# Mamba projections of a fused transformer layer: four z tiles moved into the state scans, and the order of the dt stage changed

## The reference

```python
xz = x @ in_proj_w.T
xp, z = jnp.split(xz, 2, axis=-1)
xpad = jnp.pad(xp, ((0, 0), (d_conv - 1, 0), (0, 0)))
xc = sum((xpad[:, k:k + L, :] * conv_w[:, k] for k in range(d_conv))) + conv_b
xc = jax.nn.silu(xc)
x_dbl = xc @ x_proj_w.T
dt = jax.nn.softplus(x_dbl[..., :dt_rank] @ dt_proj_w.T + dt_proj_b)
Bm = x_dbl[..., dt_rank:dt_rank + d_state]
Cm = x_dbl[..., dt_rank + d_state:]
def step(h, ts):
    dt_t, B_t, C_t, u_t = ts
    dA = jnp.exp(dt_t[..., None] * A)
    h = h * dA + (dt_t * u_t)[..., None] * B_t[:, None, :]
    y = jnp.einsum('bds,bs->bd', h, C_t)
    return (h, y)
...
y = ys.transpose(1, 0, 2) + xc * D
y = y * jax.nn.silu(z)
return y @ out_proj_w.T
```

## Time and profile before

| | |
|---|---|
| median of 3 runs | 9802.43 us (9801.89 to 9803.57) |
| the profiled execution | 9804.51 us, span 9802.8 us |
| TensorE matmul, busy | 7878.8 us, 80% |
| VectorE, busy | 7618.6 us, 78% |
| ScalarE, busy | 4259.3 us, 43% |
| GpSimd, busy | 4330.9 us, 44% |
| mean granted TensorE clock | 0.909 of full |

### The profile page before, as it was taken

The page is one execution under the profiler, slowest core; times in us unless marked ns, Lnnn a source line. Parts: engine busy times, 40 slices in busy tenths (PEclk is TensorE's granted clock), DMA queues, the critical chain, the costliest instruction groups (busy, mean ns, idle before and its releaser), DMA issues. The chain is left out here.

```text
span 9802.8 us, 98275 instructions
## 1 busy us (share of the span) xinstructions
PE 7878.8 (80%) x31796; PEld 3811.3 (39%) x31796; DVE 7618.6 (78%) x11589; ACT 4259.3 (43%) x7991; POOL 4330.9 (44%) x2631
## 2 busy tenths in 40 slices
PE   5788787887978878788887878878788787887977
PEld 2343343433434334343343434434343243432434
DVE  5787977779687696876878778787787877878777
ACT  2535435254442543525435254353534535345353
POOL 1451825418154271632726336262361724518245
PEclk8898998989989898898989889899898988989989
DMA  3020020200202002020020200102011020100202
GB/s 78 1 51 3 5 49 1 52 1 9 45 0 53 1 9 45 0 53 1 13 41 0 53 1 22 32 0 53 1 28 26 0 53 1 38 15 5 49 1 52
DMA packets 265191, 229.93 MB, mean 23 GB/s; under 512 B 26947, under 2 KB 237635, under 8 KB 264531
## 3 DMA queue, kind: packets, MB, share of 16 engines
q1 hardware_dynamic: 264678, 223.50, 10.6%
HBM read 151.60 MB, written 70.25 MB: 23 GB/s over the span
## 5 line engine op out<-in xcount | busy, mean ns | idle before, releaser
L639 POOL TENSOR_TENSOR arena<-arena 128x1024 f32<-128x1024 f32 x1024 | 2435.6, 2389 | 1312.4 <-DVE arena L1041 862.4
L778 ACT ACTIVATE PS<-arena,Aneg 128x512 f32<-128x512 f32 x2048 | 1410.5, 691 | 1628.1 <-DVE XNT L1081 883.6
L704 ACT ACTIVATE arena<-PS 128x512 f32<-128x512 f32 (+3 forms) x3072 | 1286.9, 508 | 861.4 <-PE PS L1249 856.9
L1363 PE MATMUL PS<-XNT,identf 128*128 128x512 f32 x2048 | 1012.2, 618 | 320.9 <-POOL XNT L622 320.9
L948 DVE TENSOR_REDUCE pm<-PS 128x1 f32<-128x512 f32 (+3 forms) x1728 | 1051.2, 663 | 271.5 <-PE PS L1228 169.6
L601 POOL TENSOR_SCALAR_AFFINE_SELECT arena<-arena 128x512 f32<-128x512 f32 x512 | 329.6, 644 | 2063.6 <-ACT arena L704 2063.6
L1225 PE MATMUL PS<-arena 96*128 96x512 bf16 (+3 forms) x3072 | 1105.5, 385 | 106.3 <-PEq L1447 49.4
L1363 PE MATMUL PS<-arena,identf 128*128 128x512 f32 x2048 | 1025.6, 625 | 161.9 <-DVE arena L1057 161.9
L1249 PE MATMUL PS<-arena 99*128 99x512 bf16 (+3 forms) x3072 | 894.5, 332 | 5.9
L1348 PE MATMUL PS<-arena,sel 96*128 96x512 bf16 x1664 | 513.7, 391 | 389.0 <-DVE arena L1057 319.5
L686 ACT ACTIVATE XNT<-PS 128x512 f32<-128x512 f32 x320 | 187.4, 597 | 1335.2 <-PE PS L1184 1334.5
(11 more groups left out here) (143 smaller groups left out, 13086.2 us busy)
## 6 DMA issues: line engine op xcount, KB each, us to landing
pieces_scratch<-arena SPq DMA_DIRECT2D x816, 64.0 KB
arena<-pieces_scratch SPq DMA_DIRECT2D x68, 384.0 KB, 10.0
arena<-pieces_scratch SPq DMA_DIRECT2D x85, 256.0 KB, 10.5
arena<-in_x SPq DMA_DIRECT2D x17, 1024.0 KB, 5.6
U<-in_x SPq DMA_DIRECT2D x17, 1024.0 KB, 5.6
arena<-pieces_scratch SPq DMA_DIRECT2D x136, 128.0 KB, 10.2
out<-X SPq DMA_DIRECT2D x64, 256.0 KB, 5.7
arena<-pieces_scratch SPq DMA_DIRECT2D x17, 768.0 KB
```

The source lines that it names most:

```text
L639: nc.gpsimd.tensor_tensor(DB[:, n % 2], DTU[:, j, half(th)].unsqueeze(1).to_broadcast([P, SP2, TH]), BB[:, SP2 * sg:SP2 * (sg + 1), :], AL ...
L704: A(PT[s % len(PT)][:, hh, 0:w], bank(t_bank(n))[:, 0:w], ACT.Exp, scale=DH ** -0.5)\
L778: A(bank(da_bank(m)), DT[:, j, half(th)], ACT.Exp, scale=Aneg[:, j, SP2 * sg + ss:SP2 * sg + ss + 1]).then_inc(S("dA"), 1)
L1363: ins = MM(bank(4 + jt % 2), identf[:, :], HS[k % len(HS)][:, ss, :], start=False, stop=sg == NSG - 1 and ss == SP2 - 1)
```

## The change

Z tiles 4 to 7 are no longer made ahead of the scans. TensorE makes them in steps 9, 12, 15 and 18 of the scans' loop, each after the sum of the unit before, in banks 6 and 7. ScalarE makes the tanh of each in its step n + 1, behind the two dA, and VectorE the silu in its step n + 2, behind the scans. As `in_proj` needs XNT that long, HS 2 and 3 get memory of their own (HS2), for which the selectors shrink to one column each, read 128 times. The dt stage is reordered: x projection of half 0, its four dt tiles, x projection of half 1, its four. The Ln of the first tile is an instruction of its own.

```diff
-        sel = sb("sel", [3 * 2 * DS, 2 * DS, P], BF16)
+        sel = sb("sel", [3 * 2 * DS, 2 * DS], BF16)
+        HS2 = sb("HS2", [P, 2 * SP2 * TH])
...
-            return k % 4 if k < 4 else (k + 2) % 4
+            return k % 4 if k < 4 else 6 + k % 2
...
-        DT_BANK = (6, 7, 0, 1, 2, 3, 6, 7)
+        DT_BANK = (6, 7, 0, 1, 2, 3, 0, 1)
+
+        SIDE_AT = {9: 4, 12: 5, 15: 6, 18: 7}
...
-                    pool.wait_ge(S("dtl"), nth + 1)
+                    pool.wait_ge(S("dtl"), nth + 2)
...
+            split_bc(0)
+            abs_dt(0)
+            exp_dt(0)
+            split_bc(1)
+            abs_dt(1)
+            exp_dt(1)
             spread_b(0)
-            for th in range(NTH):
-                own.wait(own.n - NTH + 1 + th)
-                A(DT[:, :, half(th)], DT[:, :, half(th)], ACT.Ln, bias=1.0).then_inc(S("dtl"), 1)
-            for k in range(4, ND * NTH):
-                tanh_z(k)
+            ln_dt(0, slice(0, 1))
+            ln_dt(0, slice(1, ND))
+            ln_dt(1, slice(0, ND))
...
                     if m < SP2:
-                        act.wait_ge(S("z"), 5 + m)
+                        act.wait_ge(S("drl"), ND + 1 + m)
...
+                if n - 1 in SIDE_AT:
+                    tanh_z(SIDE_AT[n - 1])
...
             times_u(0)
-            for k in range(4, ND * NTH):
-                silu_z(k)
-            dve.wait_ge(S("z"), ND * NTH)
...
                 dve.wait_ge(S("ys"), NSG * (jt + 1))
+                dve.wait_ge(S("z"), NTH * j + th + 1)
...
+                if n - 2 in SIDE_AT:
+                    silu_z(SIDE_AT[n - 2])
...
                 if n >= 6:
-                    pe.wait_ge(S("dab"), n - 5)
-                    pe.wait_ge(S("drl"), n - 5)
+                    pe.wait_ge(S("dab"), n - 3)
+                    pe.wait_ge(S("drl"), n - 3)
...
+            def selector(s):
+                return sel[:, s:s + 1].to_broadcast([3 * 2 * DS, P])
...
-            pe.wait_ge(S("bc"), NTH)
+            x_proj(0)
+            for n in range(ND):
+                dt_proj(n)
+            x_proj(1)
+            pe.wait_ge(S("bc"), 1)
+            pe.wait_ge(S("drl"), 2)
+            spread_b(0)
+            for n in range(ND, ND * NTH):
+                dt_proj(n)
+            spread_b(1)
             pe.wait_ge(S("drl"), ND * NTH)
-            pe.wait_ge(S("dab"), ND * NTH)
-            for k in range(4):
-                if k % 2 == 0:
-                    spread_b(k // 2)
-                in_proj(ND * NTH + 4 + k)
-            pe.wait_ge(S("z"), ND * NTH)
...
+                    if b_copied(n + 1) == NSG:
+                        pe.wait_ge(S("z"), ND * NTH)
...
+                if n in SIDE_AT:
+                    if SIDE_AT[n] == 4:
+                        pe.wait_ge(S("Be"), NSG)
+                    elif SIDE_AT[n] >= 6:
+                        pe.wait_ge(S("z"), SIDE_AT[n] - 1)
+                    in_proj(ND * NTH + SIDE_AT[n])
```

More of the change, by code:

```diff
@@ L189, in build @@
         two = [t.rearrange("p (n s t) -> p n s t", n=2, s=SP2)
-               for t in (view(28688, 2 * SP2 * TH), XNT[:, :, :].rearrange("p c t -> p (c t)"))]
+               for t in (view(28688, 2 * SP2 * TH), HS2[:, :])]
         HS = [two[0][:, 0], two[0][:, 1], two[1][:, 0], two[1][:, 1]]
@@ L197, in build @@
         TZ, TM = (view(at, 1024).rearrange("p (n t) -> p n t", n=2) for at in (28688, 13312))
+        TZ2 = view(31248, 1024).rearrange("p (n t) -> p n t", n=2)
         TC = view(24592, 4096).rearrange("p (j t) -> p j t", j=ND)
@@ L299, in _ @@
                 nc.vector.tensor_copy(mask1[:, :], mst[:, 0, :])
-                nc.vector.tensor_copy(sel[:, :, :], stage[0:3 * 2 * DS])
+                nc.vector.tensor_copy(sel[:, :], stage[0:3 * 2 * DS, :, 0])
                 nc.vector.tensor_scalar(ipw[:, :, DI:], ipw[:, :, DI:], 0.5, None, ALU.mult)
@@ L420, in dve_c, with tanh_of @@
             return not pool_c(n)
+        def tanh_of(k):
+            return (TZ if k < 4 else TZ2)[:, k % 2, :]
         def z_bank(k):
-            return k % 4 if k < 4 else (k + 2) % 4
+            return k % 4 if k < 4 else 6 + k % 2
         def row_bank(stage, i):
             return i % MB if stage == 2 else i % (2 * MB)
-        DT_BANK = (6, 7, 0, 1, 2, 3, 6, 7)
+        DT_BANK = (6, 7, 0, 1, 2, 3, 0, 1)
+        SIDE_AT = {9: 4, 12: 5, 15: 6, 18: 7}
         OUT_AT = [44 + 4 * i for i in range(NT // NTH)]
@@ L719, in tanh_z @@
                     act.wait_ge(S("z"), k - 1)
-                A(TZ[:, k % 2, :], bank(z_bank(k)), ACT.Tanh).then_inc(S("tz"), 1)
+                A(tanh_of(k), bank(z_bank(k)), ACT.Tanh).then_inc(S("tz"), 1)
             def tanh_c(m):
@@ L741, in scalar_program, with split_bc @@
             tanh_z(3)
-            for th in range(NTH):
+            def split_bc(th):
                 act.wait_ge(S("xpr"), th + 1)
@@ L745, in scalar_program, with abs_dt, exp_dt, ln_dt @@
                 A(BCP[:, half(th)], bank(4 + th)[0:SR, :], ACT.Copy).then_inc(S("bca"), 1)
[L746 to L753, removed]
+            def abs_dt(th):
+                for j in range(ND):
+                    n = th * ND + j
+                    act.wait_ge(S("dtp"), n + 1)
+                    A(DT[:, j, half(th)], bank(DT_BANK[n]), ACT.Abs, bias=dtb[:, j:j + 1]).then_inc(S("dab"), 1)
+            def exp_dt(th):
+                act.wait_ge(S("dab"), ND * (th + 1))
+                A(DT[:, :, half(th)], DT[:, :, half(th)], ACT.Exp, scale=-1.0).then_inc(S("dte"), 1)
+            def ln_dt(th, js):
+                act.wait_ge(S("dte"), th + 1)
+                A(DT[:, js, half(th)], DT[:, js, half(th)], ACT.Ln, bias=1.0).then_inc(S("dtl"), 1)
             def spread_b(k):
@@ L996, in silu_z @@
                 dve.wait_ge(S("tz"), k + 1)
-                V_.scalar_tensor_tensor(out=Z[:, m, half(th)], in0=TZ[:, k % 2, :], scalar=1.0, in1=bank(z_bank(k)),
+                V_.scalar_tensor_tensor(out=Z[:, m, half(th)], in0=tanh_of(k), scalar=1.0, in1=bank(z_bank(k)),
                                         op0=ALU.add, op1=ALU.mult).then_inc(S("z"), 1)
@@ L1024, in vector_program, with relu_dt @@
                     .then_inc(S("bc"), 1)
[L1025 to L1030, removed]
+            def relu_dt(th):
+                for j in range(ND):
+                    n = th * ND + j
+                    dve.wait_ge(S("dtp"), n + 1)
+                    dve.wait_ge(S("dab"), n + 1)
+                    V_.tensor_scalar(DTU[:, j, half(th)], bank(DT_BANK[n]), dtb[:, j:j + 1], 0.0, ALU.add, ALU.max)\
+                        .then_inc(S("drl"), 1)
+            for th in range(NTH):
+                split_bc(th)
+                relu_dt(th)
             def times_u(jt):
@@ L1291, in tensor_program, with x_proj @@
                 in_proj(n)
-            for th in range(NTH):
+            def x_proj(th):
                 for j in range(ND):
@@ L1296, in tensor_program, with dt_proj @@
                 ins.then_inc(S("xpr"), 1)
-            for n in range(ND * NTH):
+            def dt_proj(n):
                 th, j = divmod(n, ND)
@@ L1310, in spread_b @@
                     pe.wait_ge(S("Be"), k)
+                if k == 1:
+                    pe.wait_ge(S("bc"), NTH)
                 for ss in range(SP2):
-                    ins = MM(bank(6 + ss), sel[:, SP2 * sg + ss, :], BCP[:, half(th)], start=True, stop=True)
+                    ins = MM(bank(6 + ss), selector(SP2 * sg + ss), BCP[:, half(th)], start=True, stop=True)
                 ins.then_inc(S("Bg"), 1)
-            pe.wait_ge(S("bc"), NTH)
-            pe.wait_ge(S("drl"), ND * NTH)
-            pe.wait_ge(S("dab"), ND * NTH)
-            for k in range(4):
-                if k % 2 == 0:
-                    spread_b(k // 2)
-                in_proj(ND * NTH + 4 + k)
-            pe.wait_ge(S("z"), ND * NTH)
+            x_proj(0)
[8 more added lines that the diff above has]
+            spread_b(1)
+            pe.wait_ge(S("drl"), ND * NTH)
             pe.wait_ge(S("diag"), ND)
@@ L1347, in tensor_program @@
                         for ss in range(SP2):
-                            ins = MM(bank(c_bank(ss)), sel[:, DS + SP2 * sg + ss, :], BCP[:, half(th)],
+                            ins = MM(bank(c_bank(ss)), selector(DS + SP2 * sg + ss), BCP[:, half(th)],
                                      start=True, stop=True)
```

1 line of the change is left out of this document (removed), and 2 rows, old and new, of the table names.

## The result

| | before | after |
|---|---|---|
| median | 9802.6 us (9801.9 to 9803.6) | 10019.8 us (10017.4 to 10021.1) |
| ratio | | 1.0222, 95% interval 1.0209 to 1.0235 |
| profiled execution | 9804.5, span 9802.8 | 10021.1, span 10019.4 |

A forecast was written before the change was run, and what follows sets the result against it. The dt stage was taken as a latency chain through ScalarE, later scans as VectorE-bound with GpSimd close behind. Per sequence 0.1 + 11.1 + 2.7, rounded to 13.8 us, x 16 = 221 on 9802.4: 10023 us, range 9905 to 10085.

The forecast's parts named there:

- The main term: Scans with side tiles: dA stands behind a tanh waiting for TensorE's projection; with the silu, 11.1 us per sequence.
- tile 4's wait: Scan 11 waits for dA behind tanh 4, whose projection follows unit 8's sum on TensorE: +3.0 us.
- silu 4, tile 5's wait: VectorE's silu of tile 4 adds 0.6 us; scan 14 then waits through unit 11's product, TensorE and ScalarE: +1.6.
- tile 6's wait, with silu 5: Scan 17 waits through GpSimd's product of unit 14, TensorE and ScalarE: +2.5 us, silu of tile 5 hidden in it.
- silu 6, tile 7's wait: Silu of tile 6 adds 0.6 us; from unit 17's product TensorE and ScalarE add a wait of 2.2.
- sum of 0.1: ScalarE's path in the dt stage: -2.5 us (tanh moved), +0.2 (Ln piece), +2.4 (later second Exp), per sequence.
- The clock term of 2.7: TensorE at half clock after idling in the scans' stalls: +1.6 us at tile 5, +1.1 at tile 7; between 0 and 5.
- (a): Rival: the stalls in the scans as forecast, but no clock loss there: 9982 us; chance 0.12.
- (b): Rival: TensorE at full clock in the dt stage, 9974 us, chance 0.10; opposite, dt 4 to 7 at half, 10075, 0.05.
- (c): Rival: z projections held back the early scans; units 0 to 7 fall from 33.0 towards 26.8 us: 9927 us; chance 0.07.
- (d): Rival: side tiles hide fully in the scans, projection ready when ScalarE reaches tanh 4: 9754 to 9793 us; chance 0.07.
- (e): Rival: side tiles stall the scans more as halves of the clock chain up, 17 us per sequence: 10075 us; chance 0.09.

The follow-up runs named there:

- e2: New dt order alone, with z tiles 4 to 7 made ahead of the scans as in the kernel before: 9858.3 us, ratio 1.0080.
- e3: The changed kernel with the dt stage in the order of before, side tiles and early tanh as changed: 9963.5 us, ratio 1.0165.
- e11: The changed kernel with the dt matmuls over 112 rows instead of 16, zero weights for 96 of them: 9965.6 us, ratio 1.0166.
- e9: The kernel before with one added VectorE multiply per sequence, in unit 40 of the scans: 9802.7 us, ratio 1.0000.
- e4: The changed kernel with the old dt order and the side tiles' tanh and silu one unit later: 9745.3 us, ratio 0.9942 to before.
- e1: The changed kernel with ScalarE's tanh and VectorE's silu of each side tile one unit later: 9898.1 us, ratio 1.0101 to before.
- e5: e4 with the two x projections interleaved, both halves made for each block: 9746.4 us, ratio 0.9944 to the kernel before.
- e8: e5 with the dt matmuls over 112 rows instead of 16: 9720.4 us, ratio 0.9917 to the kernel before.
- e7: The kernel before with the dt matmuls over 112 rows instead of 16, zero weights for 96 of them: 9749.2 us, ratio 0.9946.
- e10: The kernel before with three added VectorE multiplies per sequence in unit 40, each waiting for the one before: 9910.3 us, ratio 1.0111.

## Why the prediction was right

**The main term: right in mechanism, place and size.** Forecast and measured starts of the scans (the first kind of sequence: what each step adds to the delay against the kernel before):

| step of the sum | forecast | measured |
|---|---|---|
| tile 4's wait | 3.0 | 2.85 |
| silu 4, tile 5's wait | 0.6 + 1.6 | 0.6 + 1.6 |
| tile 6's wait, with silu 5 | 2.5 | 3.15 |
| silu 6, tile 7's wait | 0.6 + 2.2 | 0.4 + 2.4 |
| silu 7 | 0.6 | 0.6 |
| sum | 11.1 | 11.6 |

I had called the silu of tile 5 hidden. It was hidden in the sense that scan 17 hangs on scan 14 through GpSimd, but the chain was 0.6 us longer than I had counted, 0.5 of it because TensorE came to it at half clock. Its sum of unit 14, 1.88 us at full:

```profile
445.67 2.38 PE L1409 MATMUL PS<-HS,identf 128*128 128x512 f32 x4
```

**The dt stage: right in half of the sequences.** The sum of 0.1 and its course hold in sequences 0, 2, ...: clock down under dt 2, up in the middle of x projection 1, first scan at +0.1. The last Abs and the first dA (as the earlier trace rows):

```profile
358.36 0.69 ACT L760 ACTIVATE arena<-PS,dtb 128x512 f32<-128x512 f32 x1 [1.02 <-PE PS L1340]
...
368.62 0.69 ACT L760 ACTIVATE arena<-PS,dtb 128x512 f32<-128x512 f32 x1 [0.40 <-PE PS L1340]
...
378.58 1.30 ACT L800 ACTIVATE PS<-arena,Aneg 128x512 f32<-128x512 f32 x2
```

The last Abs ends 17.9 us after the first read; 17.6 was forecast. In the others the clock was at half under dt 0 to 3 and most of x projection 1, +2.2. My bound of 3.3 for half clock had it under dt 4 to 7, which ran at full in both kinds (982.5 to 989.1 us at 1.00), and it was for all sequences at once; I had not seen that the sequences could differ. e2 confirms the late start (2.6, as forecast with the Ln piece), e3 the gain of the moved tanh (2.7 where 2.5 less 0.2 for Ln had been forecast). Two slips stand in the sum itself: the second Exp is 2.5 us late and enters as 2.4, and 13.9 is rounded to 13.8. Together they are 0.2 us per sequence, 3 us of the forecast.

**The clock term of 2.7: right in sum, wrong in place.** It was put into the stalls of tiles 5 and 7. In the changed kernel half-clock stretches followed three of TensorE's four idle gaps of 2.3 to 2.7 us there, but their records were mostly off the chain; 0.5 us was lost, at tile 6. In e11, where the stretches fall elsewhere in the scans, the stalls cost 2.4 us more, close to the 2.7. The clock's real share came in at the dt stage with the early scans (0 and 2.8, mean 1.4) and at the MLP and behind it (+2.6 and -0.6, mean 1.0), with 0.4 regained in the late scans between: together with the 0.5 about 2.5. That the clock made all of the part behind the MLP is argued from where its stretches lie, not shown. So part of the closeness of 10023 to 10020 is luck. e9 shows how much: the kernel before with 1.6 us more on the path of each sequence measures the same.

**The rivals.** (a), no clock loss, would have been right about the stalls and wrong about the sum. (b) is out in both forms: the first four dt tiles ran in part or in whole at half in both kinds, and dt 4 to 7 at full. (c) is out: units 0 to 7 took 32.9 us, and 33.5 in the second kind. (d) is out as the change stands: the projection ended 3 us too late, as its point of decision said. With a unit more of time and the old dt order it is what happens: e4 measured 9745, 9 us below the range given for (d). (e) was too high: the four waits cost what they cost one by one (9.6 us idle, 9.8 regained in e1).
The selector read as one column loads in 99 ns like the one before, at the lower bound that I took:

```profile
L1353 PEld LDWEIGHTS PS<-arena,sel x512: 97/99/152, 362.8 to 9777.3; 96*128 96x128 bf16 x171
```

The early start of unit 0 on GpSimd, for which Ln was cut, brought nothing, as the first scan waits for dA.

## What to carry to other kernels

Work that is moved beside a loop has to be ready when the engine that takes it up comes to it: find the last event that releases the producer, add the producer's queue, and compare with the moment when the consumer's next critical instruction is due. If it is short, move the consumer's step one iteration further, which cost nothing here (e1, e4). A pure latency gap is worth filling only with work whose own price in the loop, here four VectorE operations of 0.6 us in a stage that VectorE bounds, is smaller than what leaves the gap. And where TensorE's clock changes in a loop, small gains are not additive: test a change in combination, as e5 and e8 show.

## What the runs showed of the hardware

TensorE kept full clock under matmuls over 112 rows and fell to half under the same matmuls over 16, though it was busy without a gap in both cases (e7 against the earlier trace rows; e8 against e5 with next to no idle time ahead of them). Widening them with zero weights costs 5 ns in ScalarE's copy (597 against 592 ns), no TensorE time, and gains 52 us in the kernel before. The Trainium skill, TensorE: Matmul & The Clock Gate (Part 1), ties the clock to how busy the engine is; these runs show that the number of rows a matmul reads counts too. No number of rows between 16 and 112 was run.

A delay of 1.6 us per sequence disappeared by the next one (e9), and one of 6.0 grew to 6.8 (e10). At the start of the MLP the half-clock stretch is 3.2 us long in the kernel before, 6.7 in the first kind of the changed kernel, and absent in e4 and e9. A loop whose passes are all alike can settle into two kinds of passes that take turns (the changed kernel, e8).

The operation added in e9 and e10 is a VectorE multiply with both inputs in SBUF. One such (L1041) takes 0.67 us in the kernel before; the three of e10 took 2.25, 1.63 and 2.71. GpSimd was at work beside them, also with both inputs in SBUF:

```profile
523.14 2.35 POOL L639 TENSOR_TENSOR arena<-arena 128x1024 f32<-128x1024 f32 x1
...
523.79 2.25 DVE L1085 TENSOR_TENSOR arena<-arena 128x512 f32<-128x512 f32 x1
...
525.45 1.71 POOL L635 TENSOR_TENSOR arena<-arena 128x512 f32<-128x512 f32 x1
526.08 1.63 DVE L1086 TENSOR_TENSOR arena<-arena 128x512 f32<-128x512 f32 x1
527.13 2.78 POOL L639 TENSOR_TENSOR arena<-arena 128x1024 f32<-128x1024 f32 x1
527.75 2.71 DVE L1087 TENSOR_TENSOR arena<-arena 128x512 f32<-128x512 f32 x1
```

Each of the three ends 0.55 us after the GpSimd operation that was running when it started (525.49, 527.16 and 529.91), so it looks as if it could do its work only then. The other way round, L1041 at 434.39 us started first, kept its 0.67, and GpSimd's L639 beside it took 2.71 instead of 2.35. No run varies this alone.
